# Second experts, last norms and last block of a four-layer kernel: fp4 weights loaded and rounded at the experts' end, statistics joined to the sums, row and bias sums of the last block on TensorE

## The reference

```
xn = layernorm(x)
x  = x + L2_attn(xn) + L2_ffn(xn)          # L2_ffn: 16 experts, each row goes to 2 of them
xn = layernorm(x)
x  = x + L3_attn(xn) + L3_ffn(xn)

L3_attn(x):  h = layernorm(x) * g1 + b1
             a, b, c = sigmoid(h@Wa + ba), tanh(h@Wb + bb), sigmoid(h@Wc + bc)
             state_t = a_t * state_(t-1) + (1 - a_t) * b_t;   y = x + c_t * state_t
             h2 = layernorm(y) * g2 + b2
             return y + gelu(h2@W1 + bm1)@W2 + bm2
L3_ffn(x):   q(v) = v rounded to fp4 levels, with one scale (largest absolute value / 6) per 16 columns
             h = silu(q(x) @ q(w_gate).T) * (q(x) @ q(w_up).T)      # 352 columns
             return q(h) @ q(w_down).T
```

## Time and profile before

| what | us |
|---|---|
| median of 3 runs | 953.45 |
| lowest and highest run | 952.24, 964.16 |
| the profiled execution's own time | 961.29 |
| its span, first to last instruction | 959.6 |
| busy in the span: PE, DVE, ACT, POOL | 674.0, 645.9, 341.3, 377.0 |

### The profile page before, as it was taken

One profiled execution on the slowest core, in us unless ns is written; L12 is line 12 of the kernel. 1 busy time (PEld: TensorE's weight loads), 2 busy tenths in 40 slices (PEclk: granted clock), 3 DMA queues, 4 the chain that ended last, 5 costly groups with the idle time before them and its releaser, 6 DMA issues. The chain is left out here.

```text
span 959.6 us, 19016 instructions
## 1 busy us (share of the span) xinstructions
PE 674.0 (70%) x6860; PEld 516.7 (54%) x6860; DVE 645.9 (67%) x1809; ACT 341.3 (36%) x794; POOL 377.0 (39%) x513
## 2 busy tenths in 40 slices
PE   1577687788766656899999882154598771696785
PEld 1266465566545535777777682143476551353564
DVE  3763888878857573877777743836554664887886
ACT  1654111111121344666666531211113441475221
POOL 1450444444431454455655055516602662023312
PEclk9988766655669685999999997557757996597895
DMA  2000000000000400120000243364372533100000
GB/s 53 1 1 12 3 2 2 3 2 3 3 2 6 72 0 6 41 77 9 8 8 14 64 132 119 73 97 116 90 179 60 164 108 110 34 0 1 6 17 22
DMA packets 66289, 41.27 MB, mean 43 GB/s; under 512 B 11888, under 2 KB 64192, under 8 KB 66208
## 3 DMA queue, kind: packets, MB, share of 16 engines
q1 hardware_dynamic: 62432, 32.43, 14.2%
q0 software_dynamic: 3776, 7.78, 2.3%
HBM read 26.72 MB, written 13.47 MB: 42 GB/s over the span
## 5 line engine op out<-in xcount | busy, mean ns | idle before, releaser
L1733 ACT ACTIVATE l1a_weights<-l1a_score,l1a_low_top 128x128 f32<-128x128 f32 (+1 forms) x256 | 90.4, 425 | 37.9 <-DVE l1a_low_top L1765 33.9
L1765 DVE TENSOR_REDUCE l1a_low_top<-l1a_score 128x2 f32<-128x512 f32 (+1 forms) x96 | 66.1, 688 | 53.4 <-PE l1a_score L1642 52.4
L1597 POOL TENSOR_TENSOR l1a_q_of<-l1a_q_rows,l_quad_of 128x1024 fp32r<-128x1024 f32 x32 | 59.9, 1895 | 38.0 <-ACT l1a_q_rows L1722 38.0
L1277 POOL DMA_INDIRECT l_done<-l2e_done,l2r_rows x47 | 45.1, 959 | 59.3 <-DVE l2e_done L2482 58.7
L1788 DVE COPY l1a_weightsT<-l1a_flip 128x512 f32<-128x512 f32 x96 | 65.3, 680 | 0.8 <-PE l1a_flip L1677 0.7
L1639 PE MATMUL l1a_score<-l1a_k_rows,l1a_q_of 128*128 128x128 f32 (+1 forms) x256 | 53.2, 313 | 17.9 <-ACT l1a_weights L1733 10.5
L1677 PE MATMUL l1a_flip<-eye,l1a_weights 128*128 128x128 f32 x384 | 59.3, 278 | 0.1
L1639 PEld LDWEIGHTS l1a_score<-l1a_k_rows,l1a_q_of 128*128 128x128 f32 x256 | 38.4, 201 | 33.0 <-ACT l1a_weights L1733 20.5
L1677 PEld LDWEIGHTS l1a_flip<-eye,l1a_weights 128*128 128x128 f32 x384 | 47.4, 145 | 3.1 <-issue 0.8
L827 POOL TENSOR_TENSOR l0s_shared<-l0s_own,l0s_grown 128x512 f32<-128x512 f32 x16 | 18.1, 1132 | 75.3 <-ACT l0s_grown L817 75.3
L1260 POOL DMA_INDIRECT l_rows<-l2r_sent,l2r_slot x32 | 31.9, 998 | 28.6 <-DVE l2r_slot L1244 16.1
(11 more groups left out here) (545 smaller groups left out, 1968.2 us busy)
## 6 DMA issues: line engine op xcount, KB each, us to landing
l2e_wgu<-in_l_wgu SPq DMA_DIRECT2D x47, 128.0 KB, 2.1
l1e_w<-in_l_w SPq DMA_DIRECT2D x46, 128.0 KB, 2.1
l_rows<-l2r_rows SPq DMA_DIRECT2D x1, 3055.0 KB, 19.5
l2e_wd<-in_l_wd SPq DMA_DIRECT2D x47, 64.0 KB, 2.1
l2r_rows<-l_rows SPq DMA_DIRECT2D x3, 780.0 KB, 7.1
l2e_mixed<-l_done SPq DMA_DIRECT2D x8, 256.0 KB, 4.7
l_rows<-l1r_rows SPq DMA_DIRECT2D x1, 1483.5 KB, 11.6
l1r_rows<-l_rows SPq DMA_DIRECT2D x3, 387.0 KB, 3.7
```

Of the source, the lines that this page charges most:

```text
L1277: self.core.nc.gpsimd.indirect_dma_start(self.done_dram, bass.IndirectOffsetOnAxis(ap=self.rows[:, j, D:D + 1].bitcast(I32), axis=0), done ...
L1597: nc.gpsimd.tensor_tensor(q_of[i][:, 4 * g:4 * g + 4, :], rep(q_rows[:, g, :], 1, 4), rep(lat.quad_of[:, 0, 0:4], 2, L), ALU.mult).then_in ...
L1733: last = nc.scalar.activation(weights[s % 2][:, n * width:(n + 1) * width], score[s % 2][:, n * width:(n + 1) * width], ACT.Exp, bias=low_ ...
L1765: nc.vector.tensor_reduce(low_top[:, s % 2, 0:len(heads)], score[s % 2][:, :].rearrange("p (h k) -> p h k", k=key_tiles * P), AX.X, ALU.ma ...
```

## The change

- The clearing and the loading of the fp4 weights leave `layer_norm` of layer 2. POOL clears `l3q_weights` in the first attention block, ahead of its wait for the routing; SP issues the seven loads among the experts' loads, at step j == 4 of 27.
- `EARLY` goes from 9 to 7: two of the indirect DMAs go from the first attention block to the second.
- The rounding of these weights leaves the second attention block and stands, as ten instructions in a row, on DVE between the last expert tile and the sums with the returned rows (`round_weights`).
- The statistics of x are made right behind each chunk's sum in `l2_experts` (`four.x_stats`); those of y behind each chunk's add in `l3_recurrence` (`four.y_stats`); the norms only aggregate them.
- `core.xn` is made in `l3_recurrence`, eight tiles ahead of each half's rounding, no more in `l3_norms`.
- PE gets two matmuls of 512 columns in `l3_norms` whose result nobody reads (`l3a_spare`).
- The product silu * up is made in place of `up` (`join`); for the first four batches at the end of `l3_recurrence`.
- In `l3_tail` POOL's two sums are gone. `project(b)` starts each tile's sum with two more matmuls, identity x y and identity x bias2 (32 matmuls in all); `result` has two buffers, `up` two in place of three; `take_down` and `finish` come behind the rounding of a batch, and `finish` later than before.

```diff
                 order.mark(nc.vector.memset(eps_col[:, :], eps))
-                for t in range(NT):
-                    order.mark(nc.vector.bn_stats(stats[:, t, :], src[:, t, :]))
-                order.settle()
+                if made_stats is None:
+                    for t in range(NT):
+                        order.mark(nc.vector.bn_stats(stats[:, t, :], src[:, t, :]))
+                    order.settle()
...
-    EARLY = 9
+    EARLY = 7
...
                 nc.gpsimd.tensor_tensor(core.x[:, :, :], core.x[:, :, :], rep(bo[:, :], 1, NT), ALU.add).then_inc(biased, 1)
+                four.zero()
                 pool.wait_ge(shared, 2)
                 route.spread_rows(0, range(NT))
                 route.spread_rows(1, range(EARLY))
...
                     if b >= 2:
                         finish(b - 2)
-                    if b < 6:
-                        four.round_part(dve, weights_order, b)
...
                 for j in range(T - HELD):
                     sp.wait_ge(downed, j + 1)
                     gated.load(sp, route, j + HELD)
+                    if j == 4:
+                        four.issue(sp)
                 route.load_results(sp, mixed)
...
                 take_down(T - 1)
+                four.round_weights(dve, order)
                 for c in range(NC):
                     dve.wait_ge(route.loaded[c], 32)
                     rows = slice(c * TPC, (c + 1) * TPC)
                     for results in mixed:
                         order.then(nc.vector.tensor_tensor(core.x[:, rows, :], core.x[:, rows, :], results[:, rows, :], ALU.add))
+                    for t in range(c * TPC, (c + 1) * TPC):
+                        order.mark(nc.vector.bn_stats(four.x_stats[:, t, :], core.x[:, t, :]))
...
+        dve.wait_ge(self.loaded, 16 * 7)
+        fp4_scales(nc, order, weights, scale, inv)
+        fp4_levels(nc, order, weights, rep(inv, 2, BLK), level, grain)
+        order.then(nc.vector.tensor_tensor(weights, level, rep(scale, 2, BLK), ALU.mult))
+    def join(self, b):
+        return self.core.nc.vector.tensor_tensor(self.up[b][:, :, :], self.silu[b][:, :, :], self.up[b][:, :, :], ALU.mult)
...
                 for t in range(NT):
-                    order.mark(nc.vector.bn_stats(stats[:, t, :], core.x[:, t, :]))
-                order.settle()
-                for t in range(NT):
-                    last = nc.vector.bn_aggr(mean_var[:, t, :], stats[:, t, :])
+                    last = nc.vector.bn_aggr(mean_var[:, t, :], four.x_stats[:, t, :])
                     order.mark(last) if t < NT - 1 else last.then_inc(var_ready, 1)
                 dve.wait_ge(std_ready, 1)
                 order.then(nc.vector.reciprocal(rstd[:, :], std[:, :]))
                 order.then(nc.vector.tensor_tensor(left[:, :], mean_var[:, :, 1], rstd[:, :], ALU.mult))
                 nc.vector.tensor_tensor(left[:, :], left[:, :], rstd[:, :], ALU.mult).then_inc(left_ready, 1)
-                for t in range(NT):
-                    order.mark(nc.vector.tensor_scalar(core.xn[:, t, :], core.x[:, t, :], mean_var[:, t, 0:1], rstd[:, t:t + 1],
-                                                       ALU.subtract, ALU.mult))
                 dve.wait_ge(left_rooted, 1)
...
                 four.turn(pe, banks)
+                for _ in range(2):
+                    nc.tensor.matmul(spare[:, :], core.eye[:, :], core.xnT[:, 0:CH], start=True, stop=True)
...
+                    for t in range(half * NT // 2, (half + 1) * NT // 2):
+                        order.mark(nc.vector.tensor_scalar(core.xn[:, t, :], core.x[:, t, :], four.mean_var[:, t, 0:1],
+                                                           four.rstd[:, t:t + 1], ALU.subtract, ALU.mult))
+                    order.settle()
                     source = core.xn[:, half * NT // 2:(half + 1) * NT // 2, :].rearrange("p t (k e) -> p (t k) e", e=BLK)
                     level, grain = four.xlevel[:, part, :], four.xgrain[:, part, :]
                     fp4_scales(nc, order, source, four.xscale[:, part], four.xinv[:, part])
@@ -2829,9 +2831,14 @@
...
                 for c in range(NC):
+                    dve.wait_ge(kept, 2 * (c + 1))
+                    four.join(c)
                     dve.wait_ge(turned_made, c + 1)
                     rows = slice(c * TPC, (c + 1) * TPC)
                     nc.vector.tensor_tensor(y[:, rows, :], core.xn[:, rows, :], turned[c % 2][:, :, :], ALU.add).then_inc(turned_taken, 1)
+                    dve.wait_ge(turned_taken, c + 1)
+                    for t in range(c * TPC, (c + 1) * TPC):
+                        nc.vector.bn_stats(four.y_stats[:, t, :], y[:, t, :])
...
-        h, h4, h4T = sb("h", [P, TPB, W3]), pair("h4", [P, TPB, W3]), pair("h4T", [P, TPB, KT3, P])
-        UPS = 3
+        h4, h4T = pair("h4", [P, TPB, W3]), pair("h4T", [P, TPB, KT3, P])
+        UPS = 2
         up = [ps(f"up{i}", [P, CH]) for i in range(UPS)]
         down = [ps(f"down{i}", [P, TPC, D]) for i in range(2)]
-        turned, result = ps("turned", [P, TPB, TPC, P]), ps("result", [P, TPB, D])
+        turned, result = ps("turned", [P, TPB, TPC, P]), [ps(f"result{i}", [P, TPB, D]) for i in range(2)]
...
-                loads.wait(pool)
-                nc.gpsimd.tensor_tensor(y[:, :, :], y[:, :, :], rep(bias2[:, :], 1, NT), ALU.add).then_inc(added, 1)
-                pool.wait_ge(added, 1)
-                nc.gpsimd.tensor_tensor(core.x[:, :, :], core.x[:, :, :], y[:, :, :], ALU.add).then_inc(added, 1)
...
                 def project(b):
-                    pe.wait_ge(h_taken, 2 * (b + 1))
-                    if b:
-                        pe.wait_ge(whole, b)
+                    if b >= 2:
+                        pe.wait_ge(whole, b - 1)
+                    sums = result[b % 2]
                     for t in range(TPB):
+                        nc.tensor.matmul(sums[:, t, :], core.eye[:, :], y[:, b * TPB + t, :], start=True, stop=False)
+                        nc.tensor.matmul(sums[:, t, :], core.eye[:, :], bias2[:, :], start=False, stop=False)
+                        pe.wait_ge(h_taken, 2 * (b + 1))
                         for k, width in enumerate(WIDTHS):
-                            last = nc.tensor.matmul(result[:, t, :], h4T[b % 2][0:width, t, k, :], four.downT[0:width, k, :],
-                                                    start=k == 0, stop=k == KT3 - 1)
+                            last = nc.tensor.matmul(sums[:, t, :], h4T[b % 2][0:width, t, k, :], four.downT[0:width, k, :],
+                                                    start=False, stop=k == KT3 - 1)
                     last.then_inc(result_made, 1)
...
                 def take_down(c):
-                    if c == 0:
-                        dve.wait_ge(added, 2)
                     dve.wait_ge(downed, c + 1)
                     rows = core.x[:, c * TPC:(c + 1) * TPC, :]
                     nc.vector.tensor_tensor(rows, rows, down[c % 2][:, :, :], ALU.add).then_inc(taken, 1)
...
                     dve.wait_ge(result_made, b + 1)
                     dve.wait_ge(taken, b // 2 + 1)
                     rows = core.x[:, b * TPB:(b + 1) * TPB, :]
-                    nc.vector.tensor_tensor(rows, rows, result[:, :, :], ALU.add).then_inc(whole, 1)
...
+                    nc.vector.tensor_tensor(rows, rows, result[b % 2][:, :, :], ALU.add).then_inc(whole, 1)
+                finished = ((), (), (), (0,), (1,), (2,), (3, 4), (5,))
                 for b in range(B):
                     i = b % 2
-                    order.then(nc.vector.tensor_tensor(h[:, :, :], four.silu[b][:, :, :], four.up[b][:, :, :], ALU.mult))
-                    if 2 <= b < 2 + NC:
-                        take_down(b - 2)
+                    if b >= NC:
+                        order.then(four.join(b))
                     if b >= 2:
-                        finish(b - 2)
                         dve.wait_ge(h_ready, b - 1)
+                    blocks = four.up[b][:, :, :].rearrange("p t (k e) -> p (t k) e", e=BLK)
                     fp4_scales(nc, order, blocks, scale[i][:, :], inv[:, :])
                     fp4_levels(nc, order, blocks, rep(inv[:, :], 2, BLK), level[i][:, :, :], grain[:, :, :], last=False)
                     nc.vector.tensor_tensor(level[i][:, :, :], level[i][:, :, :], grain[:, :, :], ALU.subtract).then_inc(leveled, 1)
+                    if 2 <= b < 2 + NC:
+                        take_down(b - 2)
+                    for done in finished[b]:
+                        finish(done)
                 finish(B - 2)
                 finish(B - 1)
...
-                layer_norm(core, "l2_norm", core.x, route.xn, core.xnT, LN_EPS, loads=[loads, route, four], zero=[four, route])
...
-            layer_norm(core, "l3_norm2", y, inner, hT, LN_EPS, gain=norms[:, 2:3], shift=norms[:, 3:4])
```

40 lines of the change are left out of this document (15 added, 25 removed).

## The result

The changed kernel takes 924.5 us, the median of four runs (919.76 to 928.61), against 955.7 us of the kernel before in the same session (four runs, 952.24 to 964.16): a ratio of 0.967, 95% interval 0.962 to 0.971. Forecast were 929.7 us and a range of 922 to 938. The saving is 31.2 us; forecast were 23.8, taken from a median of 953.45. The profiled execution took 919.76 us, the fastest of its four, with a span of 918.0; the one of before took 961.29. The two traces take the same time up to 609.8 us.

The account below looks back on a forecast made before the run. The prediction took the bound stage by stage: SP, POOL, PE or DVE, the last two alternating in the last block. Its eight terms summed to -23.8 us, from the median 953.45 to 929.7, range 922 to 938.

Parts of the forecast that it names:

- C: Second attention block: with the rounding gone, PE's 1.43 us wait for DVE goes; -1.4 us, bounds 0 and -1.4.
- H: Last block: fewer POOL adds in DVE's way and four products moved out shorten it from 77.6 to 65.7 us; -12.0.
- fourth rival: Clock helps elsewhere: a slow stage, such as the second attention block, turns fast; 7 us more gained, 922; chance 0.04.
- A: Norm of layer 2: without the seven loads on SP the next stage starts earlier; -7.9 us, bounds -7.7 to -8.9.
- B: First attention block: two fewer row DMAs on POOL let it end earlier; -2.5 us, bounds 0 and -2.5.
- D: Experts' end: the rounding and the statistics of x added on DVE lengthen it; +2.4 us, bounds +1.4 and +4.
- E: Stage l3_norms: the statistics and the 16 operations making xn leave; -4.2 us, bounds -3.6 and -4.5.
- G: Norm of y: ACT's 3.21 us wait for the aggregates goes; -3.2 us.
- F: Recurrence: DVE gets xn, four products and 16 statistics and becomes the bound; +5.0 us, bounds +3.0 and +7.
- norm's seam: Rival: layer 2's norm end is held by something else, say the blanking DMA, so no gain there; 937.5, chance 0.07.
- last block's clock: Rival: PE's clock falls in the last block as now, leaving a gain of 4 to 5 there; 937, chance 0.12.
- slower rival: PE at the slow clock through the whole last block, 108 us against 77.6; total +19, 972; chance 0.03.

Follow-up runs that it names:

- round_late: The kernel before with only the rounding moved from the second attention block to the experts' end: 945.3 us against 957.1, ratio 0.989.
- round_back: The changed kernel with the fp4 loads and clearing back in layer 2's norm and the six-part rounding back in the second attention block: 938.8 us, ratio 0.982.
- loads_back: The changed kernel with the clearing and the seven loads of the fp4 weights back in the norm of layer 2: 935.8 us, ratio 0.976.
- gap_only: The changed kernel with the rounding's first part (four scale operations) also in the second attention block's first batch, its result unread: 933.8 us, ratio 0.981.
- early9: The changed kernel with EARLY back at 9 in place of 7: 927.8 us, ratio 0.970.
- adds_back: The changed kernel with POOL's two sums back at the last block's start and the 32 added matmuls gone: 926.8 us, ratio 0.968.
- joins_back: The changed kernel with the four first products (silu times up) back in the last block, none in the recurrence: 921.0 us, ratio 0.963.
- order_back: The changed kernel with VectorE's order in the last block as before, sum with down and finish ahead of each batch's scale: 928.0 us, ratio 0.972.

## Why the prediction was right, and where not

**The direction and the class** came from the seven terms other than C, forecast at -22.4 together and -24.8 in the two profiles. The time came out 5.2 us below the forecast and the saving 7.4 above it, and C's surplus is of that size: with the seven other terms as in the profiles, and H at its usual -10.8, 8 us of the medians' 31.2 are left for C.

**C, the term that was mis-sized.** The forecast's step read: "PE's 1.43 us wait for DVE goes; otherwise PE is busy there with or without the rounding. -1.4, bounds 0 and -1.4." The busy share hid that PE ran at 0.50, and that the same work takes 24.7 us where the clock rises early: -16.7 in the two profiled executions. Over the runs it is less, since the rise differs between executions. round_late's medians give -11.8, less +1.2 for the experts' end: -13, the surest of these figures, since both kernels ran side by side and their interval is clear of 1. round_back against loads_back gives -3, and 0.8 more for the experts' end (20.2 us against 19.4): -4, within the noise. gap_only against the changed kernel gives -9. That the rounding in this block costs several times its wait is shown; that the wait acts by putting off the clock's rise fits the five profiles that missed the early one, and isn't proved by them. The fourth rival ("without the 1.43 us gap, or after the shorter idle time, a stage that now runs slow turns fast") came nearest to it, at 7 us more and a chance of 0.04. The experiments speak for its first condition (gap_only, round_late); the second is not needed (round_late, early9).

**A** -8.6 against -7.9. The loads alone are 7.6 (loads_back). POOL started 1 us earlier, which the forecast left open; by the size that is the rest, but it wasn't tried by itself.

**B** -2.5, as said; early9 gives +2.6 back in that block and 3.3 in the medians.

**D** +2.4, as said. The meeting with the last row DMA is real (2.08 us against 0.96), and it comes back in every profile that has the rounding at the experts' end. The inference of the Trainium skill, SBUF — State Buffer, "Who interferes with whom", that descriptor building is not held up, would have made D +2.1; in each of the fourteen traces one row DMA starts 0.14 to 0.19 us behind this operation of 1.3 us, and it takes 1.96 to 2.08 us; they speak against it.

**E, G** -4.2 and -3.35 against -4.2 and -3.2. **F** +4.2 against +5.0: VectorE is busy 40.29 of 41.59 us, as forecast, and xn's second half lost 0.6 us to POOL's first products (2.76 against 2.14), as foreseen.

**H: the right size from partly wrong reasons, and by some luck.** Forecast -12.0; -12.8 in the profile, -10.8 in most. The path followed from the block's start holds up to VectorE's wait for the third sum with down (34.4 us behind the start, forecast 34.2). Behind it two errors cancel. VectorE is done at 58.9 and not 57.0 (909.06 + 0.89 less 851.02), since its products take up to 1.96 us and not 0.88. The rest takes 5.8 us and not 8.7, mainly since the forecast priced PE's last matmuls at 0.49 us each, the slow clock, and they ran fast here. "Half of this is the 7.6 us that POOL's adds cost DVE ... and most of the rest is the four products moved to F." The adds do cost VectorE 7.3 us, but the block 3.1 (adds_back), since PE's climbs and descents set the pace until the third sum with down, as the forecast's own 34.2 us had it. For the same reason the products moved are worth 0 (joins_back). The later place of VectorE's finishes is worth 5.2 (order_back), and the forecast gave it no share of its own. These sum to 8.3 of 10.8, if they may be added; the other 2.5 are open. Not tried alone were the second result bank and the clock of the block's last third, 0.50 in the trace of before (its last projection takes 2.93 us) and mostly 1.00 after. One sign was wrong too: "no DVE row there is over 1 us"; the four joins take 1.37 to 1.96. And the forecast called a wait of VectorE for PE in the last four batches a sign of being wrong, where its own sum has one: the 2.28 us stand in batch 4.

**The rivals.** The norm's seam was held by the loads and by nothing else. The last block's clock was not lower but higher, 0.97 against 0.76. The slower rival had no trace at all.

## What to carry to other kernels

A busy PE says nothing about its speed: read PEclk beside the busy share, and where it is at half for a whole stage, try to take out even a short wait of PE, which may be worth several times its length (here 1.4 us against 4 to 13), and judge by several executions, since one profile may catch an early or a late rise. Before crediting a cut on one engine, ask which engine sets the pace at that place: 7.3 us of VectorE's time were worth 3.1, and four products nothing. When an engine gets faster, the stage's next bound shows at once, here SP's loads of the rows.
